# Ten heads instead of eight find their row maxima beside the experts

## The chip, the cores and the metric

The kernel runs on one core of one Trainium2 chip. The metric is the device time of one execution in microseconds (us). TensorE does the matrix multiplications, VectorE, ScalarE and GpSimd (POOL in the profile) work on vectors, and SyncE (SP) issues most of the transfers between the memory of the chip and the core's on-chip memory (SBUF). TensorE writes its results into eight banks of PSUM, and the other engines read them from there. Engines run their own instruction streams and meet at semaphores.

## What is computed

The input x has 4 batches of 1024 tokens of width 256. The result is x plus two branches of the layer-normalized input xn:

```python
x = x + attention(xn, ...) + experts(xn, ...)

# attention: 16 heads a batch, two softmaxes a head of width 8, values of width 16
s = einsum('bnhd,bmhd->bhnm', q, k) * scale       # once for each half of the head
p = softmax(s);  a = p @ v
o = rms_norm(a1 - lam * a2) * (1 - LAMBDA_INIT)
out = o @ w_proj.T + b_proj

# experts: the two best of 8 experts for each token, capacity 1024 rows an expert
h = gelu(rows_of_expert @ w_gate)                  # 256 -> 1024
y = h @ w_down                                     # 1024 -> 256
```

With the batches there are G = 64 heads, and each has two score matrices of 1024 x 1024. A softmax subtracts the maximum of each row of the scores before the exponential. This kernel finds these maxima in a pass of its own, ahead of the pass that makes the exponentials.

## The kernel before

After a first stage (normalization, projections to q, k and v, choice of the experts) there are two long stages: the experts (about 125 to 540 us of the span) and the attention (about 540 to 1715 us). A last stage projects the output.

**Row maxima.** q and k are stored as sums of bfloat16 terms, stacked to 48 rows (STACK) for each of the two halves of a head; the halves lie at partitions 0 and 64. The maxima of a head are found in 16 pairs. A pair (`smax`, L1066 on VectorE, `smax_matmuls`, L1296 on TensorE) is two matmuls of 48 x 128 by 48 x 512 into two neighbouring banks and one VectorE reduce of 128 x 1024 over them. Pair m belongs to head m // 16. When a head has its 16 pairs, VectorE joins them (`neg_join`), GpSimd splits them into two bfloat16 terms (`neg_split`), VectorE turns them (`neg_turn`) and SyncE writes them with eight DMAs (`neg_rows_in`) as two more rows under the head's q rows, so that the score matmuls of the attention (L1314, 50 rows) subtract the maxima themselves.

**The experts' stage.** It has 16 chunks of 512 rows, two for each expert. A chunk n on TensorE is: eight gate tiles of six matmuls (L1363), alternating between banks 0 and 1; `turn_rows` (L1242), eight transposes of the next chunk's rows into banks 2 and 3; then the down matmuls (L1341 and L1343, in turn) of four tiles of 128 rows, in banks 6 and 7. ScalarE takes the gelu (L818) and a rounded copy (L820) of each gate tile, VectorE subtracts the two (L1102), which gives the low part. VectorE also makes the low parts of rows and weights (L1010, L1087) and sums the down tiles (`down_sum`, L1094). Each chunk carries eight pairs of row maxima in three visits: three pairs after gate tile 2, three after down tiles 0 and 1, two after down tile 2. Thus 8 heads (EARLY = 128 pairs) have their maxima when the attention starts. EXPERT_SMAX_PAIRS says which bank pair a pair uses, and before each the stream waits until that pair of banks is read.

**The attention stage.** It walks over the 64 heads. A head has 32 score matmuls (L1314), each followed by an exponential on ScalarE (L853), and the products with v (L1326). It goes in 16 rounds: in a round TensorE does one half of a product (eight matmuls L1326), a score, a pair of row maxima where the round carries one, and another score. `takes_pair` says which rounds carry a pair: all but round 12, and in odd heads all but rounds 4 and 12. Once a head ScalarE copies the output of the head before (`copy_o`, L836), TensorE turns it (L1406) and ScalarE takes it over (L842). The pair numbers run on from EARLY, so that the maxima are some eight heads ahead of the exponentials, and the pairs are used up during head 61.

**The ring of heads.** The stacked q and k of a head lie in a slot of `heads_qk`: four slots of their own, five in `arena_q`, which is free after the first stage, and one in `w_qk`. SyncE loads head n + 1 in chunk n while n + 1 < RING, and head g - 1 + RING in attention step g. GpSimd first sets the second half of each slot to one (`set_ones`, L563). Row maxima of head h are joined in chunk 2h + 2 or, from head 7, in the attention stage.

The order within every engine is written out by hand in the program; nothing is scheduled by a planner.

Of the kernel before, what the change touches and what calls it, by code (L numbers as in the profile page):

```python
# [10 lines left out]
BF16 = mybir.dt.bfloat16  # L11
# [10 lines left out]
TB = N // P  # L22
# [11 lines left out]
TURN_AT = 16  # L34
O_COPY_AT = 5
INVERT_AT = 12
RING = 10
EARLY = 16 * 8
VP = VW + 1
QUAD = 32  # L40
LAMBDA_INIT = 0.8 - 0.6 * float(np.exp(-0.3 * 0))
# [12 lines left out]
PARTS = 3  # L54
TILES = E * C // P
GROUP = 8
COUNT_AT, MAP_AT, ROWS_AT = 1, 11, 14
SIDES = 8
HIGH_AT = (10, 11)
# [14 lines left out]
def build_program(nc, x, w_qkv_t, w_proj_t, b_proj, lambdas, norm_w, wg, w_gate, w_down, out):  # L74
    ctx = ExitStack()
    with ctx:
# [54 lines left out]

        w_qk = sb("w_qk", [P, KC, 2 * D], F32)
        last_slot = w_qk[:].rearrange("p k n -> p (k n)").bitcast(BF16).rearrange("p (i n) -> p i n", i=2)
        heads_qk = [qk_ring[:, k] for k in range(SLOTS)] + [later_slots[:, k] for k in range(5)] + [last_slot]
        w_v_router = sb("w_v_router", [P, KC, D + E], F32)
        w_proj = sb("w_proj", [P, KC, D], F32)
        b_sb = sb("b_sb", [P, D], F32)
# [74 lines left out]
        banks = ctx.enter_context(nc.psum_tensor("banks", [P, 8, CH], F32))  # L212
        ST_BANKS = (0, 1, 7)
        SMAX_PAIRS = (2, 4)
        EXPERT_SMAX_PAIRS = (2, 4, 6, 2, 4, 0, 2, 4)
        OT_BANK = 6
        FIRST_ROWS_BANK, ROWS_BANK = 6, 2
        TURN_BANK = ST_BANKS[TURN_AT % 3]
# [109 lines left out]
        def takes_pair(t):  # L328

            g, j = divmod(t, 2 * TB)  # L330
            return j != 12 and not (j == 4 and g % 2 == 1)

        pairs_before = [EARLY]
        for t in range(2 * TB * G):
# [6 lines left out]

        def slot_after(pairs):
            return pairs_before.index(pairs)

        def join_slot(h):
            return slot_after(2 * TB * (h + 1))
# [28 lines left out]

        def smax_bank(m):

            return EXPERT_SMAX_PAIRS[m % 8] if m < EARLY else SMAX_PAIRS[m % 2]

        def ring_place(i):  # L380

# [14 lines left out]
        def _(sp):  # L396
# [99 lines left out]
            def expert_step(n):  # L496
                e, s = n // 2, n % 2
                if n + 1 < RING:
                    load_head(n + 1)
                if n < SLOTS:  # L500
                    load_v(n)
                sp.wait_ge(down_copied, 4 * n + 4)
                sp.dma_start(chunk(expert_rows, n), rows_out[:, s]).then_inc(rows_stored[s], 16)
                if s == 1 and e + 2 < E:
                    sp.wait_ge(down_psum, 4 * n + 4)
                    load_gate(e + 2, e % 2)
                    load_down(e + 2, e % 2)
                if s == 0 and e > 0:
                    neg_rows_in(e - 1)

            for n in range(2 * E):
                expert_step(n)
# [27 lines left out]
        def _(pool):  # L540
# [150 lines left out]
            def neg_split(g):  # L691

                whole = row_neg[:, g % 2, :].rearrange("p (s t) -> p s t", s=2)
                pool.wait_ge(neg_joined, g + 1)
                if g >= 2:
                    pool.wait_ge(neg_turned, g - 1)
                nc.gpsimd.tensor_tensor(neg_parts[:, g % 2, :, 0, :], whole, ones_bf[:, 0:2 * TB].rearrange("p (s t) -> p s t", s=2),  # L697
                                        ALU.mult).then_inc(neg_ready, 1)
                pool.wait_ge(neg_ready, 2 * g + 1)
                nc.gpsimd.tensor_tensor(neg_parts[:, g % 2, :, 1, :], whole, neg_parts[:, g % 2, :, 0, :],  # L700
                                        ALU.subtract).then_inc(neg_ready, 1)

            for n in range(2 * E):
                if n + 2 < 2 * E:
                    find_rows(n + 2)
                if n % 2 == 0 and n > 0:
                    neg_split(n // 2 - 1)
            for g in range(G):
                for h in late_heads:
                    if (g == 0 or invert_slot(g - 1) < join_slot(h)) and join_slot(h) <= invert_slot(g):  # L710
# [160 lines left out]
        def _(dve):  # L871
# [224 lines left out]

            def expert_step(n):
                e, s = n // 2, n % 2
                for f in range(FC):
                    dve.wait_ge(hidden_high, FC * n + f + 1)  # L1100

                    nc.vector.tensor_tensor(hidden_parts[:, LO, f, :], hidden[:, LO, f, :], hidden_parts[:, HI, f, :].bitcast(F32),  # L1102
                                            ALU.subtract).then_inc(hidden_ready, 1)
                    if n == 0 and f == 1:
                        split_low(4 * B - 1)
                    if f == 1:
                        for m in range(3):
                            smax(8 * n + m)
                    if s == 0 and e > 0 and f == 0:
                        neg_join(e - 1)  # L1110
                    if s == 0 and e > 0 and f == 4:
                        neg_turn(e - 1)
                if n + 1 < 2 * E:
                    rows_t_low(n + 1)
                if n >= 2:
                    dve.wait_ge(rows_stored[s], 16 * e)
                down_sum(n, 0)
                down_sum(n, 1)
                for m in range(3, 6):
                    smax(8 * n + m)  # L1120
                if e + 1 < E:
                    next_weights_low(n)
                smax(8 * n + 6)
                down_sum(n, 2)
                smax(8 * n + 7)
                down_sum(n, 3)
                if n == 0:
                    choice_gates()
# [61 lines left out]
        def _(pe):  # L1190
# [74 lines left out]

            def expert_smax(n, j):

                m = 8 * n + j
                if j % 8 == 0 and m % (2 * TB) == 0:
                    g = m // (2 * TB)  # L1270
                    pe.wait_ge(head_in[g % RING], HEAD_DMAS * 16 * (g // RING + 1))
                if j == 2:
                    from_first(pe, down_copied, 4 * n)
                elif j == 5:
                    pe.wait_ge(gelu_done, FC * (n + 1) + 2)
                else:
                    last_there = {0: m - 2, 1: m - 2, 3: m - 3, 4: m - 3, 6: m - 3, 7: m - 3}[j]
                    if last_there >= 0:
                        pe.wait_ge(smax_done, last_there + 3)
                smax_matmuls(m)  # L1280
# [67 lines left out]
            def expert_step(n):  # L1348
                e = n // 2
                if n % 2 == 0:  # L1350
                    if e == 0:
                        pe.wait_ge(rest_ready, 4 * B - 1)
                        pe.wait_ge(first_low, 1)
                    else:
                        pe.wait_ge(w_low, 2 * e - 1)
                pe.wait_ge(rows_t_ready, 2 * n + 2)
                if n > 0:
                    pe.wait_ge(smax_done, 8 * n)
                for f in range(FC):
                    pe.wait_ge(gelu_done, FC * n + f + 1)  # L1360
                    for c in range(KC):
                        for i, (w, r) in enumerate(TERMS):
                            mm = pe.matmul(banks[:, f % 2, :], gate_parts[e % 2][:, w, c, f * P:(f + 1) * P], rows_parts[:, r, c, :],  # L1363
                                           start=(c == 0 and i == 0), stop=(c == KC - 1 and i == len(TERMS) - 1))
                    mm.then_inc(gate_psum, 1)
                    if n == 0 and f == 2:
                        pe.wait_ge(rest_ready, 4 * B)
                    if f == 2:
                        for j in range(3):
                            expert_smax(n, j)  # L1370
                if n + 1 < 2 * E:
                    pe.wait_ge(smax_done, 8 * n + 3)
                    turn_rows(n + 1)
                if n % 2 == 0:
                    if e == 0:
                        pe.wait_ge(first_low, 2)
                    else:
                        pe.wait_ge(w_low, 2 * e)
                pe.wait_ge(smax_done, 8 * n + 5)
                for f in range(FC - 2):  # L1380
                    down_tile(n, f, 0)
                    down_tile(n, f, 1)
                for t in range(2):
                    for f in range(FC - 2, FC):
                        down_tile(n, f, t)
                if n + 1 < 2 * E:
                    pe.wait_ge(rows_t_ready, 2 * n + 4)
                for j in range(3, 6):
                    expert_smax(n, j)
                for f in range(FC):  # L1390
                    down_tile(n, f, 2)
                for j in range(6, 8):
                    expert_smax(n, j)
                for f in range(FC):
                    down_tile(n, f, 3)
# [111 lines left out]
```

## Time and profile before

| what | us |
|---|---|
| median of 3 runs | 1752.79 |
| lowest and highest run | 1752.04, 1753.38 |
| span of the profiled execution | 1749.3 |
| TensorE busy (matmuls) | 1697.2 |
| VectorE busy | 1503.2 |
| ScalarE busy | 1397.3 |
| GpSimd busy | 537.6 |

The profile is of one execution of its own, whose span goes from the first to the last instruction; the runs' times also hold what lies around the span. No other time of the profiled execution is given. In rows of the profile, PE is TensorE's matmuls, PEld its weight loads, DVE VectorE, ACT ScalarE, and L with a number a line of the kernel. Matmuls are pipelined: the start of one is at times reliable to the next start, the durations overlap.

### The profile page before, as it was taken

Reading aid. Unit: us, or ns where it says so; the run is one execution under the profiler, and the core shown is the slowest. Engines: PE = TensorE matmul, PEld = TensorE weight load, DVE = VectorE, ACT = ScalarE, POOL = GpSimd, SP = SyncE. Lnnn points to the kernel's source line nnn. Section 1 sums busy time; section 2 is a strip of 40 time slices with the busy share of each in tenths; the row PEclk is TensorE's granted clock in tenths of the full one; section 3 lists DMA queues with packets and bytes.
Section 4 is the critical chain, followed back from the end, with each engine's and each line's share of the span. In section 5 each row is a group of like instructions: output and inputs, shape, how many; then the busy total and the mean of one; then the engine's idle time right before and its main releaser. Section 6 shows DMA issues by size and latency. Waiting matters only on the chain.

```text
span 1749.3 us, 38531 instructions
## 1 busy us (share of the span) xinstructions
PE 1697.2 (97%) x15106; PEld 722.6 (41%) x15107; DVE 1503.2 (86%) x1792; ACT 1397.3 (80%) x2637; POOL 537.6 (31%) x1098
## 2 busy tenths in 40 slices
PE   6999999999999999999999999999999999999999
PEld 5557777777773222222222222222222222222227
DVE  7878787787777999999999999999999999999935
ACT  4464534544546999999999999999999999999994
POOL 1124111111000243332433323425534233443344
PEclk9989999999999999999999999999999999999999
DMA  8754333321203111111111111111111111100003
GB/s 261 219 193 137 106 105 103 107 75 54 85 25 115 34 31 41 30 37 36 29 40 32 34 32 35 38 34 33 39 30 36 36 31 39 32 22 14 11 11 103
DMA packets 92276, 109.60 MB, mean 63 GB/s; under 512 B 17472, under 2 KB 67264, under 8 KB 92096
## 3 DMA queue, kind: packets, MB, share of 16 engines
q1 hardware_dynamic: 85952, 90.36, 16.6%
q0 software_dynamic: 6144, 16.79, 3.3%
q8 instruction: 119, 1.95, 0.5%
q14 instruction: 61, 0.50, 0.1%
HBM read 72.77 MB, written 33.82 MB: 61 GB/s over the span
## 4 chain that ended last, share of the span: by engine, by line
PE 67%; ACT 28%; DVE 3%; issue 1%; DMA 1%; ACTq 0%; SPq 0%; DVEq 0%
ACT arena_t L853 25%; PE banks L1326 19%; PE banks L1314 12%; PE banks L1363 10%; PE banks L1296 8%; PE banks L1341 7%; PE banks L1343 4%; PE banks L1406 2%; ACT o_raw L836 2%; PE banks L1199 2%; PE banks L1442 1%; PE banks L1242 1%; DVE rest L951 1%; PE banks L1231 1%; DVE arena_q L958 1%
## 5 line engine op out<-in xcount | busy, mean ns | idle before, releaser
L1066 DVE TENSOR_REDUCE row_half<-banks 128x2 f32<-128x1024 f32 x1024 | 1186.5, 1216 | 81.9 <-PE banks L1296 80.0
L853 ACT ACTIVATE arena_t<-banks 128x512 f32<-128x512 f32 x2048 | 1083.2, 599 | 42.0 <-PE banks L1314 16.5
L1326 PE MATMUL banks<-arena_t,v_ring 128*17 128x256 f32 x8192 | 642.3, 386 | 25.6 <-ACT o_raw L836 25.5
L1326 PEld LDWEIGHTS banks<-arena_t,v_ring 128*17 128x17 f32 x8192 | 136.1, 95 | 408.0 <-issue 240.3
L1314 PE MATMUL banks<-arena_q 50*128 50x512 bf16 x960 | 284.1, 383 | 0.0
L1296 PE MATMUL banks<-arena_q 48*128 48x512 bf16 x960 | 268.5, 384 | 0.2 <-DVE row_half L1066 0.2
L1314 PE MATMUL banks<-qk_ring 50*128 50x512 bf16 x896 | 264.1, 385 | 1.6 <-DVE arena_r L1094 1.5
L1296 PE MATMUL banks<-qk_ring 48*128 48x512 bf16 x896 | 248.6, 382 | 0.0
L818 ACT ACTIVATE arena_t<-banks 128x512 f32<-128x512 f32 x128 | 76.6, 598 | 199.1 <-PE banks L1363 188.0
L1341 PE MATMUL banks<-w_parts,hidden_parts 128*128 128x512 f32 x512 | 186.9, 406 | 1.6 <-DVE arena_r L1094 1.6
L1363 PE MATMUL banks<-rows_parts,w_parts 128*128 128x512 f32 x768 | 183.2, 394 | 2.5 <-DVE rows_parts L1010 2.5
L1363 PEld LDWEIGHTS banks<-rows_parts,w_parts 128*128 128x128 f32 x768 | 141.8, 188 | 40.3 <-ACT arena_t L818 6.4
L697 POOL TENSOR_TENSOR neg_parts<-row_neg,ones_bf 128x16 bf16<-128x16 f32 x64 | 14.1, 220 | 450.6 <-DVE row_neg L1073 450.3
L1314 PEld LDWEIGHTS banks<-arena_q 50*128 50x128 bf16 x960 | 63.4, 93 | 202.2 <-ACT arena_t L853 174.1
L1343 PE MATMUL banks<-w_parts,hidden_parts 128*128 128x256 f32 x512 | 143.6, 280 | 0.0
L1314 PEld LDWEIGHTS banks<-qk_ring 50*128 50x128 bf16 x896 | 61.5, 93 | 193.9 <-ACT arena_t L853 163.1
L575 POOL DMA_INDIRECT arena_r<-token_rows,token_i x64 | 65.7, 1026 | 238.7 <-PE banks L1242 169.4
L600 POOL TENSOR_TENSOR inv_sum<-inv_sum,half_factor 128x16 f32<-128x16 f32 x64 | 13.8, 216 | 381.6 <-DVE inv_sum L1139 381.6
L1102 DVE TENSOR_TENSOR hidden_parts<-arena_t,hidden_parts 128x512 fp32r<-128x512 f32 x128 | 84.9, 687 | 40.4 <-ACT hidden_parts L820 40.4
L1341 PEld LDWEIGHTS banks<-w_parts,hidden_parts 128*128 128x128 f32 x512 | 96.1, 188 | 36.5 <-issue 12.7
L1343 PEld LDWEIGHTS banks<-w_parts,hidden_parts 128*128 128x128 f32 x512 | 96.7, 189 | 0.0
L820 ACT CAST hidden_parts<-arena_t 128x512 fp32r<-128x512 f32 x128 | 79.4, 620 | 4.1
(150 smaller groups left out, 1488.1 us busy)
## 6 DMA issues: line engine op xcount, KB each, us to landing
expert_rows<-arena_r SPq DMA_DIRECT2D x16, 512.0 KB, 3.2
q_stack<-arena_q SPq DMA_DIRECT2D x8, 768.0 KB, 3.5
k_stack<-arena_q SPq DMA_DIRECT2D x8, 768.0 KB, 4.4
v_ring<-v_heads SPq DMA_DIRECT2D x64, 68.0 KB, 2.9
arena_x<-x_in SPq DMA_DIRECT2D x4, 1024.0 KB, 6.3
token_rows<-arena_x SPq DMA_DIRECT2D x4, 1024.0 KB, 4.8
arena_v<-w_gate_in SPq DMA_DIRECT2D x4, 1024.0 KB, 6.3
arena_v<-w_down_in SPq DMA_DIRECT2D x4, 1024.0 KB, 8.7
```

Source lines behind the costliest of these rows:

```text
L575: nc.gpsimd.indirect_dma_start(out=rows_in[:, s, t, :], out_offset=None, in_=token_rows, in_offset=bass.IndirectOffsetOnAxis(ap=token_i[:, ...
L818: nc.scalar.activation(hidden[:, LO, f, :], banks[:, f % 2, :], ACT.Gelu).then_inc(gelu_done, 1)
L820: nc.scalar.copy(hidden_parts[:, HI, f, :], hidden[:, LO, f, :]).then_inc(hidden_high, 1)
L853: nc.scalar.activation(probs[:, kt % PSLOTS, q, :], banks[:, ST_BANKS[ring_place(i) % 3], :], ACT.Exp).then_inc(exp_done, 1)
L1066: nc.vector.tensor_reduce(halves[:, :, j // 2], banks[:, smax_bank(m):smax_bank(m) + 2, :], AX.X, ALU.max, negate=True).then_inc(smax_done, 1)
L1102: nc.vector.tensor_tensor(hidden_parts[:, LO, f, :], hidden[:, LO, f, :], hidden_parts[:, HI, f, :].bitcast(F32), ALU.subtract).then_inc(h ...
L1296: mm = pe.matmul(banks[:, smax_bank(m) + s, :], heads_qk[g % RING][rows, 0, qt * P:(qt + 1) * P], heads_qk[g % RING][rows, 1, h * CH:(h + ...
L1314: pe.matmul(banks[:, ST_BANKS[place % 3], :], heads_qk[g % RING][rows, 1, kt * P:(kt + 1) * P], heads_qk[g % RING][rows, 0, qh * CH:(qh + ...
L1326: mm = pe.matmul(banks[QUAD * q:QUAD * q + VP, OT_BANK, columns], v_ring[:, g % SLOTS, kt, :], probs[:, kt % PSLOTS, q, columns], start=(k ...
L1341: pe.matmul(banks[:, bank, :].rearrange("p (i d) -> p i d", i=2), hidden_parts[:, HI, f, tokens], weights[:, :, f, :], start=(f == 0), sto ...
L1343: mm = pe.matmul(banks[:, bank, HI * D:(HI + 1) * D], hidden_parts[:, LO, f, tokens], weights[:, HI, f, :], start=False, stop=(f == FC - 1 ...
L1363: mm = pe.matmul(banks[:, f % 2, :], gate_parts[e % 2][:, w, c, f * P:(f + 1) * P], rows_parts[:, r, c, :], start=(c == 0 and i == 0), sto ...
```

## The change

Ten heads have their maxima when the attention starts (EARLY = 160 pairs). Each chunk of the experts' stage carries ten pairs (BETWEEN) in four visits of 3, 2, 3 and 2 pairs; the added visit stands after gate tile 5. The ring has 12 slots; the two new ones lie in `rest`, which the first stage used. In the attention stage rounds 4 and 12 carry no pair in any head. Heads 0 to 8 are joined in the first chunk that starts after their last pair (`join_chunk`), and head 9 in the attention stage. `turn_rows` waits until pair 3 of the chunk is reduced, where it waited for pair 0.

```diff
-RING = 10
-EARLY = 16 * 8
+RING = 12
+EARLY_HEADS = 10
+EARLY = 2 * 8 * EARLY_HEADS
+BETWEEN = 10
...
+        rest_slots = rest[:].rearrange("p s n -> p (s n)").bitcast(BF16).rearrange("p (k i n) -> p k i n", k=2, i=2)
+        heads_qk = ([qk_ring[:, k] for k in range(SLOTS)] + [later_slots[:, k] for k in range(5)] + [last_slot]
+                    + [rest_slots[:, k] for k in range(2)])
...
-        EXPERT_SMAX_PAIRS = (2, 4, 6, 2, 4, 0, 2, 4)
+        EXPERT_SMAX_PAIRS = (2, 4, 6, 2, 4, 2, 4, 0, 2, 4)
...
         def takes_pair(t):
             g, j = divmod(t, 2 * TB)
-            return j != 12 and not (j == 4 and g % 2 == 1)
+            return j not in (4, 12)
...
+        def join_chunk(h):
+            return (2 * TB * h + 2 * TB - 1) // BETWEEN + 1
...
 # SyncE, in a chunk n (GpSimd's neg_split likewise)
-                if s == 0 and e > 0:
-                    neg_rows_in(e - 1)
+                for h in range(EARLY_HEADS - 1):
+                    if join_chunk(h) == n:
+                        neg_rows_in(h)
...
 # VectorE, in a chunk n, after the subtraction of hidden tile f
                     if f == 1:
                         for m in range(3):
-                            smax(8 * n + m)
+                            smax(first + m)
+                    if f == 4:
+                        for m in range(3, 5):
+                            smax(first + m)
...
-                for m in range(3, 6):
-                    smax(8 * n + m)
+                for m in range(5, 8):
+                    smax(first + m)
...
 # TensorE, in a chunk n, after gate tile f
                     if f == 2:
                         for j in range(3):
                             expert_smax(n, j)
+                    if f == 5:
+                        for j in range(3, 5):
+                            expert_smax(n, j)
                 if n + 1 < 2 * E:
-                    pe.wait_ge(smax_done, 8 * n + 3)
+                    pe.wait_ge(smax_done, BETWEEN * n + 6)
                     turn_rows(n + 1)
...
-                for j in range(3, 6):
+                for j in range(5, 8):
                     expert_smax(n, j)
...
-                for j in range(6, 8):
+                for j in range(8, 10):
                     expert_smax(n, j)
```

## Rows read from the trace of the kernel before

**Rows 1.** The page, part 1: busy us (share of the span) xinstructions.
```profile
PE 1697.2 (97%) x15106; PEld 722.6 (41%) x15107; DVE 1503.2 (86%) x1792; ACT 1397.3 (80%) x2637; POOL 537.6 (31%) x1098
```

**Rows 2.** Stretches: length; busy of PE, PEld, DVE, ACT, POOL; clock, DMA share, GB/s.
```profile
385.00:463.00 78.00, 78.00 (x412) 60.79 (x411) 62.01 (x75) 37.59 (x57) 12.29 (x16) 1.00 0.30 95
900.00:1100.00 200.00, 195.64 (x2111) 51.20 (x2108) 185.72 (x191) 191.72 (x371) 71.78 (x160) 1.00 0.12 34
```

**Rows 3.** Chain of waits, gate tiles 0 to 2 of three chunks: start, us, what.
```profile
228.99 4.11 PE banks L1363 x18
...
281.40 4.14 PE banks L1363 x18
...
513.47 4.14 PE banks L1363 x18
```

**Rows 4.** TensorE's timeline, chunk from 281.24 us: start, us, engine, line, operands.
```profile
286.23 7.14 PE L1363 MATMUL banks<-rows_parts,w_parts 128*128 128x512 f32 x30
...
297.44 0.28 PE L1343 MATMUL banks<-w_parts,hidden_parts 128*128 128x256 f32 x1
...
299.52 0.28 PE L1343 MATMUL banks<-w_parts,hidden_parts 128*128 128x256 f32 x1
...
300.82 0.28 PE L1343 MATMUL banks<-w_parts,hidden_parts 128*128 128x256 f32 x1
...
303.30 0.28 PE L1343 MATMUL banks<-w_parts,hidden_parts 128*128 128x256 f32 x1
...
304.38 0.28 PE L1343 MATMUL banks<-w_parts,hidden_parts 128*128 128x256 f32 x1
```

**Rows 5.** ScalarE's timeline in the attention stage, the copy once a head.
```profile
1004.10 0.59 ACT L836 COPY o_raw<-banks 128x512 f32<-128x512 f32 x1
...
1022.33 0.59 ACT L836 COPY o_raw<-banks 128x512 f32<-128x512 f32 x1
...
1040.74 0.59 ACT L836 COPY o_raw<-banks 128x512 f32<-128x512 f32 x1
...
1681.92 0.59 ACT L836 COPY o_raw<-banks 128x512 f32<-128x512 f32 x1
...
1699.20 0.59 ACT L836 COPY o_raw<-banks 128x512 f32<-128x512 f32 x1
```

**Rows 6.** VectorE and ScalarE in the same chunk; first the whole chunk as stretch.
```profile
281.24:307.12 25.88, 25.88 (x139) 20.23 (x138) 20.73 (x26) 12.53 (x19) 4.25 (x6) 1.00 0.42 138
...
286.12 3.48 DVE L1066 TENSOR_REDUCE row_half<-banks 128x2 f32<-128x1024 f32 x3
...
287.94 0.60 ACT L818 ACTIVATE arena_t<-banks 128x512 f32<-128x512 f32 x1 [1.11 <-PE banks L1363]
...
289.32 0.60 ACT L818 ACTIVATE arena_t<-banks 128x512 f32<-128x512 f32 x1
289.51 1.88 DVE L1102 TENSOR_TENSOR hidden_parts<-arena_t,hidden_parts 128x512 fp32r<-128x512 f32 x3
```

**Rows 7.** TensorE's timeline in the attention stage, the products of three rounds.
```profile
1012.82 0.63 PE L1326 MATMUL banks<-arena_t,v_ring 128*17 128x256 f32 x8
...
1013.92 0.63 PE L1326 MATMUL banks<-arena_t,v_ring 128*17 128x256 f32 x8
...
1014.80 0.63 PE L1326 MATMUL banks<-arena_t,v_ring 128*17 128x256 f32 x8
```

**Rows 8.** GpSimd's timeline, the last `set_ones`.
```profile
139.32 0.95 POOL L563 MEMSET w_qk<- 128x1024 bf16 x1
```

**Rows 9.** SyncE's timeline in a chunk: maxima of a head, a quarter head's load.
```profile
205.34 5.43 SPq L461 DMA_DIRECT2D qk_ring<-neg_blocks  x8
210.81 1.89 SPq L441 DMA_DIRECT2D arena_q<-q_stack  x3
```

**Rows 10.** Waits of the weight loads, experts' stage: us in total, times, longest.
```profile
PEld banks L1341 <- DVE arena_r L1094: 2.6, 2, 1.4
```

**Rows 11.** Stretch at the start of the attention stage, columns as in rows 2.
```profile
543.00:553.00 10.00, 9.98 (x73) 1.81 (x75) 7.74 (x7) 6.79 (x13) 0.00 (x0) 0.66 1.09 355
```

More of the change, by code:

```diff
@@ L133, in build_program @@
         last_slot = w_qk[:].rearrange("p k n -> p (k n)").bitcast(BF16).rearrange("p (i n) -> p i n", i=2)
-        heads_qk = [qk_ring[:, k] for k in range(SLOTS)] + [later_slots[:, k] for k in range(5)] + [last_slot]
+        rest_slots = rest[:].rearrange("p s n -> p (s n)").bitcast(BF16).rearrange("p (k i n) -> p k i n", k=2, i=2)
+        heads_qk = ([qk_ring[:, k] for k in range(SLOTS)] + [later_slots[:, k] for k in range(5)] + [last_slot]
+                    + [rest_slots[:, k] for k in range(2)])
         w_v_router = sb("w_v_router", [P, KC, D + E], F32)
@@ L376, in smax_bank @@
         def smax_bank(m):
-            return EXPERT_SMAX_PAIRS[m % 8] if m < EARLY else SMAX_PAIRS[m % 2]
+            return EXPERT_SMAX_PAIRS[m % BETWEEN] if m < EARLY else SMAX_PAIRS[m % 2]
         def ring_place(i):
@@ L705, in _ @@
                     find_rows(n + 2)
-                if n % 2 == 0 and n > 0:
-                    neg_split(n // 2 - 1)
+                for h in range(EARLY_HEADS - 1):
+                    if join_chunk(h) == n:
+                        neg_split(h)
             for g in range(G):
@@ L1098, in expert_step @@
                 e, s = n // 2, n % 2
+                first = BETWEEN * n
                 for f in range(FC):
@@ L1105, in expert_step @@
                         split_low(4 * B - 1)
+                    for h in range(EARLY_HEADS - 1):
+                        if join_chunk(h) == n and f == 0:
+                            neg_join(h)
+                        if join_chunk(h) == n and f == 4:
+                            neg_turn(h)
                     if f == 1:
                         for m in range(3):
-                            smax(8 * n + m)
[L1109 to L1112, printed above, removed]
+                            smax(first + m)
+                    if f == 4:
+                        for m in range(3, 5):
+                            smax(first + m)
                 if n + 1 < 2 * E:
@@ L1118, in expert_step @@
                 down_sum(n, 1)
-                for m in range(3, 6):
-                    smax(8 * n + m)
+                for m in range(5, 8):
+                    smax(first + m)
                 if e + 1 < E:
                     next_weights_low(n)
-                smax(8 * n + 6)
+                smax(first + 8)
                 down_sum(n, 2)
-                smax(8 * n + 7)
+                smax(first + 9)
                 down_sum(n, 3)
@@ L1266, in expert_smax @@
             def expert_smax(n, j):
-                m = 8 * n + j
-                if j % 8 == 0 and m % (2 * TB) == 0:
-                    g = m // (2 * TB)
+                m = BETWEEN * n + j
+                g = m // (2 * TB)
+                if m % (2 * TB) == 0:
                     pe.wait_ge(head_in[g % RING], HEAD_DMAS * 16 * (g // RING + 1))
@@ L1273, in expert_smax @@
                     from_first(pe, down_copied, 4 * n)
-                elif j == 5:
+                elif j == 7:
                     pe.wait_ge(gelu_done, FC * (n + 1) + 2)
                 else:
-                    last_there = {0: m - 2, 1: m - 2, 3: m - 3, 4: m - 3, 6: m - 3, 7: m - 3}[j]
+                    last_there = {0: m - 2, 1: m - 2, 3: m - 3, 4: m - 3, 5: m - 2, 6: m - 2, 8: m - 3, 9: m - 3}[j]
                     if last_there >= 0:
@@ L1357, in expert_step @@
                 if n > 0:
-                    pe.wait_ge(smax_done, 8 * n)
+                    pe.wait_ge(smax_done, BETWEEN * n)
                 for f in range(FC):
@@ L1378, in expert_step @@
                         pe.wait_ge(w_low, 2 * e)
-                pe.wait_ge(smax_done, 8 * n + 5)
+                pe.wait_ge(smax_done, BETWEEN * n + 5)
                 for f in range(FC - 2):
```

## The prediction

> **What bounds the kernel now.** I read the page's totals first: TensorE is busy 97% of the span, VectorE 86%, ScalarE 80% [rows 1]. Such shares are means over stages, so the second view is the stretches by stage [rows 2]. In the experts' stage (125 to 541 us) the reader is to see TensorE busy 78.00 of 78 us, VectorE 62.01, ScalarE 37.59: TensorE has no slack there. In the attention stage they are 195.64, 185.72 and 191.72 of 200 us: three engines near full, and a share doesn't say which one paces. The third view, the chain of waits, gives the length of an expert chunk [rows 3]: nine steps from 281.40 to 513.47 make 25.79 us each, and the two steps from 228.99 to 281.40 make 52.4, 0.8 us too much. The fourth, TensorE's timeline, prices a visit of row maxima inside a chunk [rows 4]. In the fifth, ScalarE's timeline of the attention stage, the copy of the output (L836) stands once a head and is a ruler: its starts are 18.23 and 18.41 us apart in turn [rows 5].
>
> **The change in parts.** Total work stays: 1024 pairs (two matmuls L1296 and one VectorE reduce L1066 each). 32 pairs move from the attention stage into the 16 chunks, two to a chunk.
>
> *1. Two pairs more and one visit more in each chunk, on TensorE.* In the down stream L1343 starts every 0.35 us (297.44 to 299.52, six steps). Across the three-pair visit the starts are 299.52 and 300.82, so 1.30, 0.96 more than one step; across the two-pair visit 303.30 and 304.38, so 1.08, 0.73 more [rows 4]. The difference, 0.23 us, is a pair; the other 0.27 us is paid for entering and leaving, whatever is inside. The change keeps visits of 3, 3 and 2 pairs and adds a fourth, of 2 pairs, after gate tile 5: 0.73 us. Beside VectorE's reduces TensorE's steps are also a little longer: 0.354 us (300.82 to 303.30, seven steps) against 0.347 (297.44 to 299.52), 2%; two reduces more last 2.3 us, so 0.05 us. Sum: 16 x 0.78 = 12.5 us. Nothing hides it [rows 2]. Lower bound: the two pairs alone, 16 x 0.46 = 7.4. Upper bound: the price of a three-pair visit, 16 x 0.96 = 15.4.
> The page "TensorEngine Tiling (Array Packing)" of the Trainium skill, section Key Properties, says that changing the tiling mode, and not merely the tile, drains TensorE. The expert matmuls use all 128 rows, the pairs 48 rows from partitions 0 and 64; the fixed 0.27 us of a visit agrees with that rule. It speaks against this change, since the pairs are taken from between scores that are in their mode already; without the rule this part would be the 7.4 us.
>
> *2. VectorE in a chunk.* Two more reduces of 1.16 us (three in 3.48 us) come after the subtraction of hidden tile 4 [rows 6]. In the chunk from 281.24 us VectorE is busy 20.73 of 25.88 us [rows 6], idle 5.2, so 2.3 fit. Queued behind them are the subtractions of tiles 5 to 7, then rows_t_low; the down stream needs tile 5 only five double steps (3.5 us) after its start. One new wait can bite: turn_rows now waits until the chunk's pair 3 is reduced, as it shares banks 2 and 3. TensorE makes that pair at about 291.0 (286.23, 18 of 30 matmuls of a 7.14 us row, a first pair of 0.4 us) [rows 4]; VectorE ends tiles 2 to 4 at 289.51 + 1.88 = 291.4 [rows 6], plus a turn of 0.2 in nine chunks; pair 3 is done at 292.7. TensorE ends its gate stream at 293.2 [rows 4], with the new visit 294.0: 1.3 us to spare, cost nothing. If that cover went, all lateness past 1.3 us would be paid 16 times.
>
> *3. The attention stage.* An even head has one round without a pair (12), an odd one two (4 and 12). 18.41 us belong to heads with 15 pairs, 18.23 to 14 [rows 5], so the fifteenth pair costs 0.18 us. Upper bound: TensorE's round is 1.10 us with a pair (1012.82 to 1013.92) and 0.88 without (to 1014.80) [rows 7], 0.22. Lower bound: with no pairs at all the ruler reads 17.28 us (1681.92 to 1699.20) [rows 5], so the other 14 are worth 0.95 together, 0.07 each. Now all heads have 14. The pairs run out in head 61 both times (896 / 14.5 = 61.8 heads, 864 / 14 = 61.7), so 31 even heads lose one pair, and head 61 has 10 in place of 11. Gain: 32 x 0.18 = 5.8 us, from 2.2 to 7.0. I take the middle because it is read from this very difference, the ruler of whole heads.
>
> *4. Loads and memsets.* Two more set_ones memsets, 0.95 us each on GpSimd [rows 8], go ahead of find_rows(2), whose rows are used a chunk later: nothing. Heads 10 and 11 are loaded in chunks 9 and 10, 12 DMAs each. On SyncE eight neg DMAs take 5.43 us and three load DMAs 1.89 [rows 9], so the worst chunk issues 5.4 + 4 x 1.9 and some 2 us of stores and weights: 15 of 26.6 us. Past them are queued the row store and the next expert's weights, used two chunks later: nothing. In the attention stage each head is loaded two heads earlier than before, by the same number of DMAs: nothing.
>
> **Sum.** 12.5 - 5.8 = +6.7 us. The profiled execution spans 1749.3 us; the median of the runs is 3.5 us above, which I take as what lies around the span. The span becomes 1756.0 and the time 1752.8 + 6.7 = 1759.5 us, +0.38%.
>
> **What may move by itself.** In two chunks TensorE's weight loads wait 2.6 us in all for down_sum L1094, 0.8 us a chunk of it on the path [rows 3, 10]. I have no cause for it; it can vanish or strike more often: -1.6 to +2. At the start of the attention stage TensorE's granted clock is 0.66 over 543 to 553 us [rows 11], that is 2.4 GHz with a stretch of 1.2 GHz in it, at the change of stages. At most 3.4 us of full-rate time are lost there. With other starting times the stretch may be absent or longer: -2 to +1.
>
> **Rivals.**
> A. *The added visit is hidden* (the other side). In the gate stream TensorE and ScalarE alternate over two banks, and ScalarE starts its gelus 1.38 us apart (287.94, 289.32) [rows 6], TensorE needs 6 of 30 matmuls of 7.14 us, 1.4 us [rows 4]. If ScalarE were the pacer, the visit would fall into TensorE's waiting. The change wins once a chunk costs under 5.8 / 16 = 0.36 us; at 0.1 us it gives 1752.8 + 1.6 - 5.8 = 1748.6. Against: the 30 gate matmuls run on without a gap and no faster after the first visit, as they would if they had been waiting.
> B. *VectorE becomes late for turn_rows* or for the last pairs of a chunk. For: 20.7 + 2.3 = 23 us of a 26.6 us chunk. Against: the 1.3 us. At 0.5 us a chunk: 1759.5 + 8 = 1767.5.
> C. *The attention stage gives nothing back*: all heads with 14 pairs are paced by something that 15-pair neighbours hid. 1752.8 + 12.5 = 1765.3. Against: the ruler alternates alike from head to head.
>
> **How the numbers follow.** Forecast 0.79; A, B and C 0.07 each. The forecast's own range is 1755 to 1763 (the bounds of the visit and of the pair, the two odd waits, the clock). For 80% over all cases: 1754 to 1765. A measurement of this kernel tells about 0.2% (3.5 us) from no change: faster is under 1749.3, slower over 1756.3. A gives 0.05 faster and 0.02 the same; the forecast's low end 0.01 and 0.12. So 0.06, 0.14, 0.80.
>
> **What would show it.** Right: chunk starts 26.6 us apart; a fourth L1296 visit of four matmuls a chunk; the ruler at 18.23 us in every head until 61; VectorE near 23 us in a chunk and no wait for L1066 ahead of L1242. Wrong: chunks under 26.2 us (A), waits of L1242 on L1066 (B), heads over 18.3 us (C).

## The result and the profile after

The changed kernel takes 1756.65 us (median, 1755.32 to 1759.7) against 1752.05 us (1750.75 to 1753.38) of the kernel before on the same chip: a ratio of 1.0027, 95% interval 1.0018 to 1.0036. It is slower by 4.6 us; I had forecast slower by 6.7 us. The profiled execution took 1755.32 us, 2.1 more than its span, so what lies around a span is nearer 2 us than the 3.5 that I took.

The page of the changed kernel, its span, totals and chain by line. Line numbers are shifted: L1378 is the gate matmul (before L1363), L1311 the pair (L1296), L1076 its reduce (L1066), L1356 and L1358 the down matmuls (L1341, L1343), L1341 the products with v (L1326), L846 the copy once a head (L836), L863 the exponential (L853), L1257 the transposes of `turn_rows` (L1242), L1104 down_sum (L1094).

```profile
span 1753.2 us, 38534 instructions
...
PE 1701.5 (97%) x15107; PEld 726.3 (41%) x15107; DVE 1501.0 (86%) x1792; ACT 1393.1 (79%) x2637; POOL 537.9 (31%) x1100
```

The totals have hardly moved [rows 1]; what moved is inside the stages. The same two stretches as in rows 2:

```profile
385.00:463.00 78.00, 78.00 (x413) 59.65 (x412) 66.72 (x79) 37.57 (x57) 12.60 (x16) 1.00 0.31 98
900.00:1100.00 200.00, 195.65 (x2110) 52.58 (x2108) 180.24 (x185) 191.97 (x374) 66.98 (x155) 1.00 0.12 35
```

VectorE went from 62.01 to 66.72 us in the experts' 78 us, and from 185.72 to 180.24 in the attention's 200 [rows 2]. TensorE was full in the first stretch and still is, so what was put there can only make it longer. The chain of waits gives the chunks:

```profile
123.63 4.35 PE banks L1378 x18
...
283.92 4.14 PE banks L1378 x18
...
311.49 4.14 PE banks L1378 x18
...
523.96 4.14 PE banks L1378 x18
```

Eight chunks from 311.49 to 523.96 make 26.56 us each, where they made 25.79 [rows 3]: 0.77 us more. One chunk (283.92 to 311.49) has 27.57 us, 1.0 us too much. As in the two long chunks of the kernel before, TensorE waits there for a late down_sum (L1104, 1.5 us at its weight load); why VectorE is late is open. ScalarE's timeline gives the heads, in the middle and at both ends of the attention stage:

```profile
551.56 4.03 ACT L863 ACTIVATE arena_t<-banks 128x512 f32<-128x512 f32 x8 [12.07 <-PE banks L1329]
...
573.49 0.59 ACT L846 COPY o_raw<-banks 128x512 f32<-128x512 f32 x1
...
993.29 0.59 ACT L846 COPY o_raw<-banks 128x512 f32<-128x512 f32 x1
...
1011.52 0.59 ACT L846 COPY o_raw<-banks 128x512 f32<-128x512 f32 x1
...
1029.76 0.59 ACT L846 COPY o_raw<-banks 128x512 f32<-128x512 f32 x1
...
1703.10 0.59 ACT L846 COPY o_raw<-banks 128x512 f32<-128x512 f32 x1
```

The 18.41 us of every second head [rows 5] are gone: 18.23 and 18.24. To cut the whole span at the same places, the kernel before needs two more rows: its first exponentials and its first copy.

```profile
540.30 3.54 ACT L853 ACTIVATE arena_t<-banks 128x512 f32<-128x512 f32 x7 [12.07 <-PE banks L1314]
...
563.97 0.59 ACT L836 COPY o_raw<-banks 128x512 f32<-128x512 f32 x1
```

| piece of the span | before | after | difference |
|---|---|---|---|
| start to gate tile 0 of chunk 0 (124.83; 123.63) | 124.83 | 123.63 | -1.2 |
| to the same place of chunk 15 (513.47; 523.96) | 388.64 | 400.33 | +11.7 |
| to the first exponential (540.30; 551.56) | 26.83 | 27.60 | +0.8 |
| to the first copy, that is head 0 and six exponentials (563.97; 573.49) | 23.67 | 21.93 | -1.7 |
| to the copy in head 63 (1699.20; 1703.10) | 1135.23 | 1129.61 | -5.6 |
| to the end | 50.1 | 50.1 | 0 |
| span | 1749.3 | 1753.2 | +3.9 |

Two pieces answer to the two terms of my sum: +12.5 us in the 16 chunks, against 12.5 forecast; -5.6 us in the heads, against 5.8 forecast. The others, -1.2 and -1.7, I had not in the sum. That 12.5 meets 12.5 is in part luck: the price of 0.77 us makes 12.3 in 16 chunks, and the odd waits, which the forecast did not put into this term, nearly cancel here. The kernel before has two long chunks (1.6 us together), the changed one has its long chunk (1.0 us) and 0.9 us too much in its first two chunks, of which the kernel before has 0.2.

### The profile page after: what moved, and what is told of

It reads as the page before. It is cut to its first block, busy times and chain, and to the rows that moved or that the text cites. A ratio compares the mean times of both kernels' runs of the same rounds, so it can differ in the third digit from the quotient of the medians.

```text
span 1753.2 us, 38534 instructions
## 1 busy us (share of the span) xinstructions
PE 1701.5 (97%) x15107; PEld 726.3 (41%) x15107; DVE 1501.0 (86%) x1792; ACT 1393.1 (79%) x2637; POOL 537.9 (31%) x1100
## 4 chain that ended last, share of the span: by engine, by line
PE 66%; ACT 28%; DVE 4%; issue 1%; DMA 1%; ACTq 0%; SPq 0%; DVEq 0%
ACT arena_t L863 26%; PE banks L1341 19%; PE banks L1329 11%; PE banks L1378 10%; PE banks L1311 8%; PE banks L1356 7%; PE banks L1358 3%; PE banks L1424 2%; ACT o_raw L846 2%; PE banks L1214 2%; PE banks L1460 1%; PE banks L1257 1%; DVE rest L961 1%; DVE row_half L1076 1%; PE banks L1246 1%
## 5 line engine op out<-in xcount | busy, mean ns | idle before, releaser
L1076 DVE TENSOR_REDUCE row_half<-banks 128x2 f32<-128x1024 f32 x1024 | 1187.2, 1216 | 109.8 <-PE banks L1311 105.1
L863 ACT ACTIVATE arena_t<-banks 128x512 f32<-128x512 f32 x2048 | 1079.2, 600 | 38.7 <-PE banks L1329 15.0
L1341 PE MATMUL banks<-arena_t,v_ring 128*17 128x256 f32 x8192 | 641.7, 385 | 25.6 <-ACT o_raw L846 25.5
L1341 PEld LDWEIGHTS banks<-arena_t,v_ring 128*17 128x17 f32 x8192 | 136.3, 95 | 391.8 <-issue 235.2
L1329 PE MATMUL banks<-arena_q 50*128 50x512 bf16 x800 | 233.8, 383 | 0.0
L1329 PE MATMUL banks<-qk_ring 50*128 50x512 bf16 x768 | 223.5, 385 | 1.6 <-DVE arena_r L1104 1.5
L1311 PE MATMUL banks<-arena_q 48*128 48x512 bf16 x800 | 215.2, 382 | 0.0
L1311 PE MATMUL banks<-qk_ring 48*128 48x512 bf16 x768 | 210.6, 382 | 0.0
L1378 PE MATMUL banks<-rows_parts,w_parts 128*128 128x512 f32 x768 | 188.0, 397 | 0.4 <-DVE rows_parts L1020 0.4
L1356 PE MATMUL banks<-w_parts,hidden_parts 128*128 128x512 f32 x512 | 187.1, 406 | 1.0 <-DVE arena_r L1104 1.0
L1378 PEld LDWEIGHTS banks<-rows_parts,w_parts 128*128 128x128 f32 x768 | 140.5, 188 | 44.2 <-issue 8.4
L1358 PE MATMUL banks<-w_parts,hidden_parts 128*128 128x256 f32 x512 | 143.7, 281 | 0.0
L1329 PEld LDWEIGHTS banks<-arena_q 50*128 50x128 bf16 x800 | 54.4, 93 | 170.8 <-ACT arena_t L863 141.5
L1329 PEld LDWEIGHTS banks<-qk_ring 50*128 50x128 bf16 x768 | 53.9, 93 | 168.4 <-ACT arena_t L863 136.6
L1356 PEld LDWEIGHTS banks<-w_parts,hidden_parts 128*128 128x128 f32 x512 | 96.2, 188 | 35.7 <-issue 12.5
L1358 PEld LDWEIGHTS banks<-w_parts,hidden_parts 128*128 128x128 f32 x512 | 96.8, 189 | 0.0
L1311 PE MATMUL banks<-rest 48*128 48x512 bf16 x320 | 95.7, 384 | 0.2 <-DVE row_half L1076 0.2
```

Source lines behind the costliest of these rows:

```text
L863: nc.scalar.activation(probs[:, kt % PSLOTS, q, :], banks[:, ST_BANKS[ring_place(i) % 3], :], ACT.Exp).then_inc(exp_done, 1)
L1076: nc.vector.tensor_reduce(halves[:, :, j // 2], banks[:, smax_bank(m):smax_bank(m) + 2, :], AX.X, ALU.max, negate=True).then_inc(smax_done, 1)
L1311: mm = pe.matmul(banks[:, smax_bank(m) + s, :], heads_qk[g % RING][rows, 0, qt * P:(qt + 1) * P], heads_qk[g % RING][rows, 1, h * CH:(h + ...
L1329: pe.matmul(banks[:, ST_BANKS[place % 3], :], heads_qk[g % RING][rows, 1, kt * P:(kt + 1) * P], heads_qk[g % RING][rows, 0, qh * CH:(qh + ...
L1341: mm = pe.matmul(banks[QUAD * q:QUAD * q + VP, OT_BANK, columns], v_ring[:, g % SLOTS, kt, :], probs[:, kt % PSLOTS, q, columns], start=(k ...
L1356: pe.matmul(banks[:, bank, :].rearrange("p (i d) -> p i d", i=2), hidden_parts[:, HI, f, tokens], weights[:, :, f, :], start=(f == 0), sto ...
```

## The experiments

Line numbers in each kernel differ by a few from those above. Chunk steps are read from the chain of waits as above, heads from the copy once a head. Each ratio is against the kernel before on the same chip.

**One visit more, no pair more.** Kernel before, its eight pairs in visits of 2, 1, 3 and 2.

```diff
 # TensorE; VectorE reduces pair 2 after the subtraction of tile 4 likewise
                     if f == 2:
-                        for j in range(3):
+                        for j in range(2):
                             expert_smax(n, j)
+                    if f == 5:
+                        expert_smax(n, 2)
...
```

> The kernel before, with its eight pairs a chunk in four visits (2, 1, 3, 2) where it has three (3, 3, 2): one visit more, no pair more. Theory (a visit has a fixed price of 0.27 us, for entering and leaving): each chunk 0.27 us longer, so +4.3 us in all, about 1756.4; attention unchanged. Rival 1 (only pairs cost, the visit itself is free): 0. Rival 2 (the visit falls into waits of TensorE on ScalarE's gelu): 0 or below.

Measured: ratio 1.0029 (1.0017 to 1.0040), 1753.14 against 1748.02 us. The chain:

```profile
306.63 4.14 PE banks L1365 x18
...
515.37 4.14 PE banks L1365 x18
```

Eight steps in 208.74, 26.09 us each, 0.30 more than before; the ruler of the heads alternates as before. So 16 x 0.30 = 4.8 us for nothing but entering and leaving, beside 5.1 us by the runs. Both rivals fall; my 0.27 us was 10% low.

**What in the visit costs.** Two more kernels: the kernel before with one added piece of work after gate tile 5, read by nobody.

```diff
+                    if f == 5:
+                        pe.wait_ge(smax_done, 8 * n + 3)
+                        pe.matmul(banks[:, 2, :], ones_bf[:, 0:P], ones_bf[:, 0:CH], start=True, stop=True)
```

```diff
+                    if f == 5:
+                        pe.wait_ge(smax_done, 8 * n + 3)
+                        for s in range(2):
+                            rows = slice(HALF * s, HALF * s + STACK)
+                            pe.matmul(banks[:, 2 + s, :], ones_bf[rows, 0:P], ones_bf[rows, 0:CH], start=True, stop=True)
```

> The kernel before, with one more matmul a chunk after gate tile 5: ones, bfloat16, all 128 rows, 128 x 512 into bank 2, read by nobody. Theory (the fixed price of a visit is the change between 128 rows and 48-row halves, with a drain each way): the chunk grows by the matmul alone, 0.22 us, to 26.02. Rival (the fixed price is that of leaving the 32-bit matmuls for bfloat16, or of the wait at that place): 0.5 us as for the pair, to 26.3.

> The same, with a pair of 48-row matmuls of ones at partitions 0 and 64 into banks 2 and 3 in place of the full one. Both theories: 0.23 us for the pair and 0.27 us for the visit, 0.5 us together, chunk 26.3. If it is as cheap as the full matmul, the tiling is not what costs.

Measured in one execution each: 1751.25 us with the full matmul, 1758.63 with the pair, 1747.31 for the kernel before on that chip. One execution each can't price 16 x 0.3 us by its time, so I read the chain. The full matmul first, then the pair:

```profile
306.24 4.14 PE banks L1363 x18
...
514.82 4.14 PE banks L1363 x18
```

```profile
178.03 4.14 PE banks L1363 x18
...
362.43 4.14 PE banks L1363 x18
```

8 steps in 208.58 us, 26.07 each, with the full matmul; 7 steps in 184.40, 26.34 each, with the pair. Over 25.79 these are 0.28 and 0.55 us. The gate stream itself says it directly: 30 matmuls that took 7.14 us [rows 4] take 7.42 in the first kernel,

```profile
285.06 7.42 PE L1363 MATMUL banks<-rows_parts,w_parts 128*128 128x512 f32 x30
```

(the trace has no record of the added matmul, but of its weight load in all 16 chunks). In the second the row is cut by the pair, and 12 matmuls follow 0.32 us behind its start:

```profile
288.24 4.42 PE L1363 MATMUL banks<-rows_parts,w_parts 128*128 128x512 f32 x18
292.59 0.39 PE L1375 MATMUL banks<-ones_bf 48*128 48x512 bf16 x2
292.91 3.02 PE L1363 MATMUL banks<-rows_parts,w_parts 128*128 128x512 f32 x12
```

A pair streams the same 512 columns as the full matmul, in the same type, at the same place and behind the same wait, and costs 0.27 us more. That it is two instructions doesn't explain this: a further pair inside a visit costs 0.23 us [rows 4], less than the one full matmul. So going from 128 rows to the 48-row halves and back is worth 0.27 us a visit. Over the 0.23 us of a pair the full matmul costs 0.05 us, which I put down to leaving the 32-bit stream (by the difference, not by a run of its own), and the pair 0.32 us, the whole fixed price. What TensorE does in that time no row shows. The Trainium skill, "TensorEngine Tiling (Array Packing)", Key Properties, states that drain without a size; the runs agree with it.

**The fifteenth pair.** The changed kernel with the rounds of before.

```diff
-            return j not in (4, 12)
+            return j != 12 and not (j == 4 and g % 2 == 1)
```

> The changed kernel, with the attention rounds of the kernel before (even heads 15 pairs, odd heads 14). The experts' stage is that of the change. Theory (the fifteenth pair of a head costs 0.18 us, and a head without pairs is 17.28): 30 even heads at 18.41, +5.4; the pairs run out in head 59 and heads 60 and 61 fall to 17.3, -1.9; together +3.5 us on the changed kernel, 1760. Rival (heads of 14 pairs are only fast beside heads of 15, or the fifteenth pair is free in a row): no alternation of 18.41 and 18.23.

Measured: ratio 1.0064 (1.0050 to 1.0078) to the kernel before. The ruler in the middle, and in heads without pairs:

```profile
1013.79 0.59 ACT L846 COPY o_raw<-banks 128x512 f32<-128x512 f32 x1
...
1032.02 0.59 ACT L846 COPY o_raw<-banks 128x512 f32<-128x512 f32 x1
...
1050.43 0.59 ACT L846 COPY o_raw<-banks 128x512 f32<-128x512 f32 x1
...
1654.50 0.59 ACT L846 COPY o_raw<-banks 128x512 f32<-128x512 f32 x1
...
1671.77 0.59 ACT L846 COPY o_raw<-banks 128x512 f32<-128x512 f32 x1
```

18.23 and 18.41 are back, and 17.27 us stand where no pair is. From the first copy (573.75) to that in head 63 (1706.32) it takes 1132.57 us, 3.0 more than the changed kernel's 1129.61, with 3.5 forecast. By the timed ratios the distance is 6.5 us (1.0064 against 1.0027, whose intervals leave 2.4 to 10.5). They are from different chips, and there the kernel before differs: 1748.02 us on this chip (10), 1747.31 on chip 14 (one execution), 1752.05 and 1752.01 in the other two sets of runs. None of the six profiles taken on chips 10 and 14 has a long chunk of the late down_sum; the profiles of the kernel before from the other sets have two and three (1.6 and 2.0 us), those of the changed kernel one each. So ratios from different chips are not to be subtracted. The changed kernel itself was not run on chip 10 or 14; by the prices alone it would be some 7 us slower there, which is an estimate (16 x 0.77 - 5.6, and the first two chunks).

**The mirror.** Two pairs and a visit cost a chunk 0.77 us, and the same two pairs cost the attention stage 0.36, so the gain lies the other way: six heads beside the experts, in two visits of three.

```diff
 # against the changed kernel
-RING = 12
-EARLY_HEADS = 10
+RING = 10
+EARLY_HEADS = 6
...
-BETWEEN = 10
+BETWEEN = 6
...
-        EXPERT_SMAX_PAIRS = (2, 4, 6, 2, 4, 2, 4, 0, 2, 4)
+        EXPERT_SMAX_PAIRS = (2, 4, 6, 2, 4, 0)
...
-            return j not in (4, 12)
+            return j != 12
...
```

with the visits after gate tile 5 and after down tile 2 taken out on both engines.

> The mirror of the change: six heads have their maxima beside the experts, six pairs a chunk in two visits of three, ring of 10, all attention heads with 15 pairs. Theory: the two-pair visit goes, -0.78 us a chunk, -12.5; 30 odd heads go from 18.23 to 18.41, +5.4; together -7 us on the kernel before, 1745. Rival (what moves the time is the difference of stalls and not the prices, so that any step off the tuned point costs): not under 1752. Rival 2 (heads of 15 in a row let VectorE fall behind, since 15 x 1.13 us and 0.6 us are near 18.4): heads over 18.41, gain under 4.

Measured: ratio 0.9974 (0.9963 to 0.9984), 1743.39 against 1748.02 us: faster than the kernel before by 4.6 us instead of 7. The chunks are as forecast, the heads not quite. The chunks, then the ruler in the middle and at one of three longer heads:

```profile
200.02 4.09 PE banks L1372 x18
...
425.12 4.08 PE banks L1372 x18
```

```profile
992.09 0.59 ACT L845 COPY o_raw<-banks 128x512 f32<-128x512 f32 x1
...
1010.50 0.59 ACT L845 COPY o_raw<-banks 128x512 f32<-128x512 f32 x1
...
1176.29 0.59 ACT L845 COPY o_raw<-banks 128x512 f32<-128x512 f32 x1
...
1194.99 0.59 ACT L845 COPY o_raw<-banks 128x512 f32<-128x512 f32 x1
```

Nine steps make 25.01 us each (0.78 less), and heads 18.41. But three of the odd heads grow by 0.47 us and not by 0.18 (one is the 18.70 shown), and head 61 by 0.52. From the first copy (549.77) to that in head 63 (1691.86) it takes 1142.09 us against 1135.23: 6.9 us more, where I had forecast 5.4. With 12.4 us less in the chunks the parts make -5.5 us, beside the -4.6 of the runs on one chip. (Its span, 1741.7, is 7.6 us under the 1749.3 of before, but that is a profile from another chip, with two long chunks.) So the mechanism holds, with a somewhat dearer fifteenth pair; a rival that puts every departure from the tuned point at a loss falls. Why the three heads are longer is open; rival 2, VectorE falling behind, holds at most for them.

**Further the same way.** Three heads, one visit of three, every round with a pair.

```diff
 # against the changed kernel
-RING = 12
-EARLY_HEADS = 10
+RING = 10
+EARLY_HEADS = 3
...
-BETWEEN = 10
+BETWEEN = 3
...
-        EXPERT_SMAX_PAIRS = (2, 4, 6, 2, 4, 2, 4, 0, 2, 4)
+        EXPERT_SMAX_PAIRS = (2, 4, 6)
...
-            return j not in (4, 12)
+            return True
...
```

> Further the same way: three heads beside the experts, three pairs a chunk in one visit, every attention round with a pair (16 a head, 61 heads). Theory: the chunks lose 0.96 + 0.73 + 0.12 = 1.8 us each, -29; in the attention stage VectorE becomes the bound, 16 x 1.131 + 0.6 = 18.7 us a head against a mean of 18.32, +25; together about -4. Rival (the sixteenth pair costs 0.18 us like the fifteenth): 80 pairs at 0.18 = +14, together -15, heads at 18.6.

Measured: ratio 1.0054 (1.0041 to 1.0068), 1757.73 against 1748.02 us: slower by 9.7 us, where I expected 4 us less. The heads are nearly as forecast, the chunks not. The ruler, the attention stretch, three chunks of the chain, then TensorE between down tiles 1 and 2 and its wait over 200 to 500 us:

```profile
1011.30 0.59 ACT L845 COPY o_raw<-banks 128x512 f32<-128x512 f32 x1
...
1030.10 0.59 ACT L845 COPY o_raw<-banks 128x512 f32<-128x512 f32 x1
```

```profile
900.00:1100.00 200.00, 197.19 (x2092) 50.44 (x2092) 196.40 (x203) 189.04 (x363) 66.38 (x151) 1.00 0.12 34
```

```profile
419.36 4.12 PE banks L1370 x18
...
492.99 4.12 PE banks L1370 x18
```

```profile
290.19 0.28 PE L1350 MATMUL banks<-w_parts,hidden_parts 128*128 128x256 f32 x1
...
290.72 0.47 PE L1348 MATMUL banks<-w_parts,hidden_parts 128*128 128x512 f32 x1 [0.26 <-DVE arena_r L1103]
...
PE banks L1348 <- DVE arena_r L1103: 3.0, 12, 0.3
```

A head takes 18.80 us with VectorE busy 196.40 of 200: it is the bound there, 0.39 us for the sixteenth pair where the fifteenth costs 0.18. The 16 chunks give back 20 us and not 29: a chunk takes 24.54 us, 1.25 less than before, not 1.8. With no visit between the down tiles, the first matmul of tile 2 (L1348) starts 0.53 us behind the last of tile 1, where 0.12 is usual in that stream, and it waits for down_sum in each of the 12 chunks. The visits had covered that wait. I had costed only their price and not what they hid. The heads take 1163.59 us against 1135.23, 28 us more, with 25 forecast; together 8 us, near the 9.7 of the runs.

**The border of the stages.** TensorE's granted clock has a stretch at the lower level, 1.2 GHz, in head 0 of every kernel so far [rows 11]; ahead of it TensorE stood idle for 1.50 us, waiting for the last down_sum, and then did the first scores and pairs of head 0 at 2.4 GHz. Two kernels fill TensorE's wait for the last down_sum with matmuls of ones into bank 1: seven of them, in the changed kernel and in the six-heads kernel.

```diff
+FILLERS = 7
...
+            pe.wait_ge(smax_done, EARLY - BETWEEN + 7 + 3)
+            for i in range(FILLERS):
+                pe.matmul(banks[:, 1, :], ones_bf[:, 0:P], ones_bf[:, 0:CH], start=True, stop=True)
             pe.wait_ge(down_copied, 8 * E)
```

(`5 + 3` in the six-heads kernel, which waits for the same reduce. The recorded expectation says five matmuls there; it does seven too.)

> The changed kernel; between the two stages, where TensorE waits for the last down_sum, it does seven matmuls of ones (128 x 128 by 128 x 512) into bank 1, which nobody reads. Theory (the stretch of 1.2 GHz at the start of the attention stage follows from TensorE's thin work at the border of the stages): granted clock full from 120 us to the end, head 0 near 18.4 us in place of 18.8 to 20.5, so 0.4 to 2 us less than the changed kernel. Rival (the stretch comes from head 0 itself, whose first rounds have no products): the stretch stays, time as the changed kernel.

> Six heads in two visits (the kernel that was 0.26% faster than before), with five such matmuls at the border of the stages. Theory: head 0 falls from 20.4 to near 18.5 us, so 2 us less, about 0.9963 of the kernel before. Rival: as without the fill, 0.9974.

Measured: the changed kernel with the fill 1.0024 (1.0015 to 1.0033), no different from 1.0027; six heads with the fill 0.9943 (0.9929 to 0.9956), 1742.17 against 1752.01 us, the fastest of all. Its distance to the 0.9974 without the fill is no measure of the fill, since the two stand against the kernel before on two chips; in their own times the two are 1.2 us apart (1742.17 and 1743.39). Stretches of 10 us at the same place: the changed kernel, then it with the fill, then six heads, then those with the fill.

```profile
555.00:565.00 10.00, 10.00 (x94) 2.00 (x86) 8.25 (x9) 8.16 (x17) 0.00 (x0) 0.83 0.81 256
```

```profile
557.00:567.00 10.00, 10.00 (x94) 2.01 (x86) 8.25 (x9) 8.16 (x17) 0.00 (x0) 0.83 0.80 259
```

```profile
528.00:538.00 10.00, 9.77 (x67) 1.66 (x64) 7.84 (x7) 6.90 (x14) 0.24 (x2) 0.66 1.07 347
```

```profile
528.00:538.00 10.00, 9.64 (x89) 2.42 (x89) 10.00 (x10) 9.38 (x19) 0.44 (x2) 1.00 1.04 326
```

In the six-heads kernel the low stretch is gone, and from the first exponential to the first copy it is 20.80 us in place of 23.56:

```profile
527.70 4.03 ACT L863 ACTIVATE arena_t<-banks 128x512 f32<-128x512 f32 x8 [11.35 <-PE banks L1324]
...
548.50 0.59 ACT L846 COPY o_raw<-banks 128x512 f32<-128x512 f32 x1
```

```profile
526.21 3.54 ACT L862 ACTIVATE arena_t<-banks 128x512 f32<-128x512 f32 x7 [11.35 <-PE banks L1323]
...
549.77 0.59 ACT L845 COPY o_raw<-banks 128x512 f32<-128x512 f32 x1
```

In the changed kernel the fill did nothing to it. Whether it is the fill or the chance of the start that removed the stretch in the one case stays open; the theory holds in one of two. That TensorE's wait ahead of head 0 is the cause is not shown: the changed kernel with the fill has no such wait and has the stretch.

**Both kernels once more.**

> The changed kernel once more, unaltered, on the chip of the two fills. By the prices read so far it is 16 x 0.77 - 5.6 = 6.7 us over the kernel before where the first pair of profiles differed by 3.9 us, of which -1.2 lay ahead of the first chunk and -1.75 in head 0. Theory (these two and the 0.8 us stalls vary from execution to execution): the chunks and the heads from 1 on as in the first profile to 0.1 us, the start of chunk 0 and head 0 at other values. Rival (they belong to the change): 123.6 and 18.76 again.

> The kernel before, unaltered, one more profile. Theory (varies from execution to execution): the two chunks of 26.6 us elsewhere or absent, the start of chunk 0 and head 0 at other values than 124.83 and 20.51, heads 1 to 62 at 1135.4 us again. Rival (they belong to the kernel): the same values.

Measured: the changed kernel 1.0028 (1.0017 to 1.0039), 1756.79 against 1752.01 us; the kernel before 1753.04 in its one execution. Chunk 0 starts at 125.11 in it and at 125.91 in the kernel before, against 123.63 and 124.83 in the first profiles; spans are 1754.9 and 1750.9. The kernel before has three long chunks this time, the changed one again one and again the longer first two, and head 0 again the clock of 0.66; the changed kernel has it now too:

```profile
553.00:563.00 10.00, 9.90 (x66) 1.88 (x66) 7.43 (x8) 7.89 (x15) 0.43 (x2) 0.66 0.55 180
```

```profile
544.00:554.00 10.00, 9.79 (x72) 1.71 (x71) 7.74 (x8) 6.79 (x14) 0.00 (x0) 0.66 1.08 346
```

The pieces of this pair, cut at the same places:

| piece of the span | before | after | difference |
|---|---|---|---|
| start to chunk 0 | 125.91 | 125.11 | -0.8 |
| to chunk 15 (514.91; 524.71) | 389.00 | 399.60 | +10.6 |
| to the first exponential (541.74; 552.31) | 26.83 | 27.60 | +0.8 |
| to the first copy (565.41; 575.06) | 23.67 | 22.75 | -0.9 |
| to the copy in head 63 (1700.64; 1704.75) | 1135.23 | 1129.69 | -5.5 |
| to the end | 50.3 | 50.1 | -0.1 |
| span | 1750.9 | 1754.9 | +4.0 |

So the start of chunk 0 moves by 2 us from execution to execution and belongs to neither kernel: the kernel before with one full matmul a chunk, which differs from it only behind that place, has 123.63 too. The stretch of the clock varies in one and the same kernel, and the short one is not the change's own either: the kernel before with one full matmul a chunk has it (545 to 548 us), and there head 0, cut as in the tables, takes 22.19 us in place of 23.67.

## Why the prediction was right

- *Price of a visit and of two pairs.* 0.78 us a chunk forecast, 0.77 measured, so 12.5 and 12.3 for 16 chunks. The split into a price of the pairs and a fixed one was right, with the fixed one too small: 0.27 us forecast, 0.30 and 0.32 by two independent edits. The lower bound (pairs alone) is excluded.
- *The 0.05 us beside VectorE's reduces.* I had this wrong, and it made up for the fixed price. In the chunk of the kernel before that follows the one I read, TensorE's steps in tiles 0 and 1 are 0.354 us as well (15 steps, 320.03 to 325.34), and beside them VectorE does no reduce of row maxima:

```profile
320.03 0.28 PE L1343 MATMUL banks<-w_parts,hidden_parts 128*128 128x256 f32 x1
...
325.34 0.28 PE L1343 MATMUL banks<-w_parts,hidden_parts 128*128 128x256 f32 x1
...
320.00:325.30 5.30, 0.00 (x0) 1.00 0.39 123
```

The last line is the stretch with the reduces of L1066 alone, of which there is none. What makes the step 0.347 in one chunk and 0.354 in the next is open.

- *VectorE's room.* Right for 14 of 16 chunks: VectorE's 66.72 of 78 us are 22.8 of a 26.6 us chunk, and no transpose waits for a reduce there. In the first two chunks the new wait did bite, 0.4 us in chunk 0 and 0.7 in chunk 1. Between 123 and 178 us of the changed kernel:

```profile
PEld banks L1257 <- DVE row_half L1076: 1.1, 2, 0.7
```

I had worked the 1.3 us of cover from a chunk in the middle (1.5 by the rows, since 286.23 and 7.14 make 293.4 and not 293.2). In chunk 0 VectorE is behind: it begins the reduces of pairs 3 and 4 11.6 us after the chunk's start (135.23), and 10.0 us after it in the chunk from 338.07. The two chunks are 0.9 us too long, 0.7 more than in the kernel before, and all four profiles with ten pairs a chunk have this: the mechanism of rival B, without its weight.
- *Attention.* 0.18 us a head forecast, in 31 heads and a last one: 5.8; measured 5.6. Rival C falls with the ruler.
- *Loads and memsets.* No wait of TensorE or VectorE between 123 and 551 us names one of them.
- *Rival A* falls with the chunks and once more with the four visits of eight pairs.
- *What the sum missed.* 6.7 us forecast, 4.6 and 4.8 by two sets of runs, 3.9 and 4.0 by two pairs of profiles. The two terms hold (12.3 - 5.6 = 6.7), so what is missing lies in what I had put at 0 in the sum, and it is made up differently in each pair. In the first it is the start of chunk 0 (-1.2), head 0 (-1.7, with a granted clock of 0.83 over 10 us where the kernel before has 0.66) and the long chunks (one against two, -0.6); in the second the start (-0.8), head 0 (-0.9) and the long chunks (one against three, -1.3). Against them stand +0.7 us in the first two chunks of both. Head 0 and the long chunks are the two things of which I had said that they may move by themselves. That the missing 2 us have the same size in both sets of runs says that the change may have a part in them; the profiles don't show it.

## What to carry to other kernels

Work moved between two saturated stages is worth the difference of its prices, and these are read off before any run: from the spacing of instruction starts across the inserted piece at the old place and at the new. Small packed matmuls between full ones cost a fixed amount for each visit (0.30 us here), so put many into few visits, or leave them among others of their kind. Before a visit is taken out, ask what wait it covers. And compare a kernel only with runs of the other on the same chip: the kernel before differs by 4 us between two chips here, as much as the whole effect.

## What was not expected of the hardware

TensorE's granted clock falls to a mean of 0.66 over 10 us at the start of the attention stage (a part at 1.2 GHz, the rest at 2.4) though TensorE is recorded busy for 9.8 to 10 of them, in one and the same kernel at times 0.83, and in one variant not at all. It costs head 0 up to 2.8 us (23.56 against 20.80, of two executions). And a pair beyond the point where VectorE is full costs 0.39 us where the one before it cost 0.18: 18.23, 18.41 and 18.80 us for 14, 15 and 16 pairs in most heads, 17.27 for none.
